# Attention networks of a recurrent mixture kernel: token shift through DRAM, plain transposes, two buffers of the transposed input, feed-forward steps later in the round

## Chip, cores and metric

The kernel runs on one core of a Trainium2 chip. The metric is device time in microseconds (us) from launch to end; lower is better. The kernel before takes 8431.38 us (median of 3 runs, 8424.31 to 8488.79).

## What is computed

Four layers of mixers and feed-forward networks run one after the other on a stream of 8 sequences of 512 tokens with 128 features (4096 tokens in all). The change touches two of the eight networks, both stacks of local attention: L0f (16 heads, 6 layers deep, windows of 32 keys) and L1f (8 heads, 2 layers deep, windows of 64). One layer of either is, cut to what matters:

```python
def shift_tokens(t):                       # half of the features comes from the token before
    a, s = jnp.split(t, 2, -1)
    s = jnp.pad(s, ((0, 0), (1, 0), (0, 0)))[:, :-1]
    return jnp.concatenate([a, s], -1)

x = x + attn_layer(shift_tokens(x), Wqkv, q_scale, k_scale, Wo)
x = x + ffn_layer(shift_tokens(x), ln_g, ln_b, W1, b1, W2, b2)

def attn_layer(x, ...):                    # heads of 64 features
    q, k, v = jnp.split(x @ Wqkv, 3, -1)
    q, k = l2norm(q) * qs, l2norm(k) * ksc
    q, k = rotary(q), rotary(k)            # cos and sin times a position scale
    return local_attention(q, k, v) @ Wo   # a window sees itself and the window before

def ffn_layer(x, g, bln, W1, b1, W2, b2):
    xn = (x - mu) / jnp.sqrt(var + 1e-05) * g + bln
    a, gate = jnp.split(xn @ W1 + b1, 2, -1)
    return a * jax.nn.gelu(gate) @ W2 + b2
```

So each layer shifts tokens twice: the input of the attention, and the input of the feed-forward part.

## The kernel before

The stream of all tokens stays in SBUF as `g.f` (in the profile `f`): 128 partitions (the token within its tile) by 32 tiles by 128 features; a sequence is 4 tiles (`TT = 4`). L0f is `narrow_attention_net`, L1f is `local_attention_net`; their structure is one. Each has three stages: "before" (the first projections), "main" and "after" (the feed-forward part of the last sequence). The main stage makes a round for every layer and sequence: 48 rounds in L0f, 16 in L1f. A round goes over the 4 tiles tt = 0 to 3.

The order of TensorE's work in a round is written out by hand: `ORDER` names the steps of one tile (projections q, k, v; `turn`, the transposes of q and k; `score`, `flip`, the transposes of the probabilities; `value`; `out`, the product with Wo), and `SIDE` names the steps that come once per round and where: `(("fshift",), (0, 1))` puts the step at place 1 of tile 0. Places 0, 1 and 2 of a tile are at its start, after `out` of the tile before, and ahead of `value` of the first group (L0f) or of `flip` (L1f). The orders of VectorE (DVE), ScalarE (ACT) and GpSimd (POOL) are worked out from TensorE's by a small model (`in_order`): a step's `TOOK` moves the clock, and what an engine does for a step is placed at a delay from `LATER` behind it. Each engine then runs its list in order, and semaphores do the rest.

Steps have a lag. `shift`, and the projections of tiles 0 and 1, work for the next sequence; the feed-forward steps `fshift`, `fturn`, `gate` 0 to 2, `up` 0 to 2, `down` work for the sequence before. Products that are read once go through a ring of 3 PSUM banks, given out in the order of use (`Banks`): a step waits until the one three uses earlier has been read.

Token shift for the attention: POOL copies the next sequence from `g.f` to `xb` (L748; step `fetch`). TensorE makes the transposed, shifted input with 12 matmuls (L1005 to L1007; in L1f L1788 to L1790): per tile one with the identity for the features that stay, one with `down1` (a matrix that moves tokens by one place) and one with `last1` (which brings the last token of the tile before). ACT copies the bank to `hT` (L799, L1580), the only buffer, and so waits first until the last projection of the sequence in work has been written. Token shift for the feed-forward part (step `fshift`): three matmuls on `g.f` (L1094 to L1096; L1887 to L1889), which wait for VectorE's addition of `out` of tile 3 (L956, L1739: `f <- ring, f`); VectorE copies the result to `xn` (L961, L1744) and takes its mean and variance with BN_STATS and BN_AGGR; POOL makes `rstd`, ACT normalises `xn` (L854, L1633), TensorE transposes it (`fturn`, L1101, L1894), ACT applies gain and bias into `hnT` (L860, L1639), and the gates follow (L1108, L1901).

SyncE (SP) has the DMA queue. In a round of L0f it issues 30 transfers that gather shifted windows of v into `vmix` (`mix`, L692 to L695): 6 for tile 0, 8 for each other tile. In a round of L1f it issues 6 (L1477, L1478). Each `mix` waits for the projections of v of its tile. SP also loads the weights of the next layer. In the stage "before" it issues rope, mask, ln and wqkv at once, beside POOL's memsets.

## Time and profile before

| | |
|---|---|
| Median of 3 runs | 8431.38 us (8424.31 to 8488.79) |
| Profiled execution, its own time | 8455.97 us |
| Span of its instructions | 8454.1 us |
| L0f, from its first to its last projection copy to hT | 666.1 to 4660.6 us |
| L1f, the same | 5704.6 to 6633.1 us |
| TensorE busy over the span | 80% |
| TensorE clock granted in L0f / in L1f | 0.99 / 0.94 |

How to read it: engine names are PE (TensorE matmul), PEld (its weight load), DVE (VectorE), ACT (ScalarE), POOL (GpSimd), SPq (SyncE's DMA issues). L1018 is line 1018 of the kernel. A fp32 matmul stands in the trace as two instructions, a transpose as one. Busy time of a group is the time in which at least one of it runs, so the sums of lines that alternate (as L1005 to L1007 do) count the same time more than once; a window with only these instructions gives their common time. A granted clock of 1.00 is 2.4 GHz and 0.50 is 1.2 GHz.

### The profile page before, as it was taken

The numbers are of one execution on the slowest core, as the hardware profiler recorded it, in microseconds if no ns is written. First come the engines' busy times: TensorE is split into PE (matmuls) and PEld (weight loads), VectorE is DVE, ScalarE is ACT, GpSimd is POOL, SyncE is SP. The second block draws the span as 40 slices with busy tenths as digits, with TensorE's granted clock in tenths as the row PEclk, the third lists the DMA queues.
The fourth block names the chain that finished last, engine by engine and source line by source line (L and its number), as shares of the span: only waits on it lengthen the run. The fifth ranks groups of instructions, "written<-read, shape, count | busy, mean of one in ns | idle before, by whom it ended". The sixth has DMA issues, their size and how long they took to land. (4 is left out here: it accounts for less than half of the span.)

```text
span 8454.1 us, 243652 instructions
## 1 busy us (share of the span) xinstructions
PE 6789.6 (80%) x92884; PEld 4792.7 (57%) x92884; DVE 5620.9 (66%) x11929; ACT 4975.8 (59%) x10706; POOL 4197.0 (50%) x3732
## 2 busy tenths in 40 slices
PE   5777999999999999999999599987888577633267
PEld 2325666666666666666666488885555323323245
DVE  6895776777677677677677377766667488735332
ACT  4545777777777777777777344436767554302122
POOL 4555665666566566566666245554444355430000
PEclk8888999999999999999999699998999788866578
DMA  3221111111111111111111200000000132321001
GB/s 126 120 98 52 40 41 50 40 38 49 42 41 49 41 38 48 42 41 46 43 41 39 74 5 5 6 13 22 15 23 16 39 146 108 149 68 52 21 0 30
DMA packets 234165, 413.24 MB, mean 49 GB/s; under 512 B 41944, under 2 KB 125360, under 8 KB 214128
## 3 DMA queue, kind: packets, MB, share of 16 engines
q1 hardware_dynamic: 225344, 377.76, 14.2%
q8 instruction: 742, 12.16, 0.6%
q10 hardware_dynamic: 1584, 15.21, 0.4%
q0 software_dynamic: 6144, 5.25, 0.4%
q14 instruction: 351, 2.88, 0.1%
HBM read 208.61 MB, written 32.18 MB: 28 GB/s over the span
## 5 line engine op out<-in xcount | busy, mean ns | idle before, releaser
L763 POOL TENSOR_TENSOR L0f_qr<-L0f_qs,L0f_table 128x512 f32<-128x512 f32 x776 | 989.2, 1275 | 461.9 <-ACT L0f_qs L804 358.9
L1018 PE MATMUL L0f_ring<-L0f_wqkv,L0f_hT 128*128 128x512 f32 x2324 | 1173.3, 611 | 42.2 <-ACT L0f_hT L799 37.5
L770 POOL TENSOR_TENSOR L0f_qr<-L0f_qr,L0f_m 128x512 f32<-128x512 f32 x776 | 984.9, 1269 | 162.2 <-issue 106.5
L834 ACT ACTIVATE L0f_scores<-L0f_scores,L0f_nmx,L0f_rn 128x64 f32<-128x64 f32 x3072 | 982.5, 400 | 132.0 <-DVE L0f_nmx L939 130.8
L1075 PEld LDWEIGHTS L0f_o<-L0f_pT,L0f_vmix 64*64 64x64 f32 x18480 | 759.1, 137 | 158.7 <-issue 136.0
L1075 PE MATMUL L0f_o<-L0f_pT,L0f_vmix 64*64 64x32 f32 x18480 | 801.4, 221 | 50.6 <-ACT L0f_pT L842 31.8
L1075 PE MATMUL L0f_o<-L0f_pT,L0f_vb 64*64 64x32 f32 x6160 | 750.6, 221 | 0.7 <-issue 0.4
L777 POOL TENSOR_TENSOR L0f_qr<-L0f_qr,L0f_rn 128x512 f32<-128x512 f32 x388 | 396.3, 1042 | 687.7 <-DVE L0f_rn L931 686.4
L908 DVE TENSOR_TENSOR L0f_m<-L0f_ring,L0f_table 128x512 f32<-128x512 f32 x776 | 524.0, 685 | 254.9 <-ACT L0f_qs L804 246.3
L1075 PEld LDWEIGHTS L0f_o<-L0f_pT,L0f_vb 64*64 64x64 f32 x6160 | 604.3, 137 | 2.3 <-issue 2.3
L916 DVE TENSOR_REDUCE L0f_ssq<-L0f_sq 128x8 f32<-128x512 f32 x776 | 509.6, 675 | 76.7 <-ACT L0f_sq L809 71.9
L804 ACT ACTIVATE L0f_qs<-L0f_ring 128x512 f32<-128x512 f32 x776 | 474.0, 611 | 140.2 <-PE L0f_ring L1018 131.7
L1018 PEld LDWEIGHTS L0f_ring<-L0f_wqkv,L0f_hT 128*128 128x128 f32 x2324 | 384.7, 191 | 287.5 <-issue 234.4
L1025 PE MATMUL L0f_ring<-const_ident,L0f_qr 128*128 128x128 f32 x3088 | 486.4, 280 | 49.4 <-DVE L0f_m L908 44.5
L850 ACT ACTIVATE L0f_oT<-L0f_o 128x512 f32<-128x512 f32 x385 | 238.1, 618 | 472.6 <-PE L0f_o L1075 472.6
L1025 PEld LDWEIGHTS L0f_ring<-const_ident,L0f_qr 128*128 128x128 f32 x3088 | 355.6, 141 | 282.9 <-issue 184.4
L809 ACT ACTIVATE L0f_sq<-L0f_qs 128x512 f32<-128x512 f32 x776 | 484.9, 646 | 3.6 <-DVE L0f_ssq L916 3.2
L1085 PEld LDWEIGHTS L0f_ring<-L0f_wo,L0f_oT 128*128 128x128 f32 x3088 | 373.3, 197 | 118.9 <-issue 118.9
L2100 POOL TENSOR_TENSOR L0a_dbu<-L0a_du,L0a_bc_all 128x512 f32<-128x512 f32 x256 | 319.7, 1270 | 231.8 <-DVE L0a_da L2218 201.1
L2100 POOL TENSOR_TENSOR L2a_dbu<-L2a_du,L2a_bc_all 128x512 f32<-128x512 f32 x256 | 319.2, 1268 | 231.2 <-DVE L2a_da L2218 199.6
L1085 PE MATMUL L0f_ring<-L0f_wo,L0f_oT 128*128 128x128 f32 x3088 | 393.3, 282 | 0.8 <-ACT L0f_oT L850 0.8
L945 DVE TENSOR_REDUCE L0f_sums<-L0f_scores 128x8 f32<-128x512 f32 x384 | 265.5, 691 | 192.6 <-ACT L0f_scores L834 181.1
(538 smaller groups left out, 17117.0 us busy)
## 6 DMA issues: line engine op xcount, KB each, us to landing
L0f_vmix<-L0f_vb SPq DMA_DIRECT2D x768, 128.0 KB, 2.5
L0a_bc_all<-L0a_bc_rows SPq DMA_DIRECT2D x32, 2048.0 KB, 11.4
L2a_bc_all<-L2a_bc_rows SPq DMA_DIRECT2D x32, 2048.0 KB, 11.3
L0f_vmix<-L0f_vb SPq DMA_DIRECT2D x672, 64.0 KB, 2.0
L1f_vmix<-L1f_vb SPq DMA_DIRECT2D x96, 128.0 KB, 2.4
L0f_wqkv<-L_ffn_wqkv_dram SPq DMA_DIRECT2D x7, 1536.0 KB, 6.2
L2f_parts<-L2f_zero ACTq DMA_DIRECT2D x8, 1088.0 KB, 11.4
n_s<-mixer_out SPq DMA_DIRECT2D x32, 256.0 KB, 5.0
```

The source lines that it names most:

```text
L763: e.tensor_tensor(rotated, qs[:, q % QN], spread(cos, 1, 8), ALU.mult).then_inc(cosed.sem, 1)
L770: e.tensor_tensor(rotated, rotated, m2[:, q % SN], ALU.add).then_inc(added.sem, 1)
L804: e.activation(qs[:, q % QN], ring.at(step)[:], ACT.Copy).then_inc(copied.sem, 1)
L809: e.activation(sq[:, q % SN], qs[:, q % QN], ACT.Square).then_inc(squared.sem, 1)
L834: a = e.activation(s_ps[:, s, h, j], s_ps[:, s, h, j], ACT.Exp, bias=nmx[:, s, col:col + 1], scale=rn[:, tt, 2 * u, col:col + 1])
L908: e.tensor_tensor(m2[:, q % SN].rearrange("p h (a d) -> p h a d", a=2), swapped, spread(sin, 1, 8).rearrange("p h (a d) -> p h a d", a=2), ...
L916: e.tensor_reduce(ssq[:, tt % 2, slot(step)], sq[:, q % SN], AX.X, ALU.add).then_inc(summed.sem, 1)
L1018: e.matmul(bank[:], hT[:, tt * P:tt * P + P], wqkv[:, layer % 2, col:col + 512], start=True, stop=True).then_inc(full, 1)
L1025: a = e.transpose(bank[:, j * P:j * P + P], qr[:, tt % 2, 2 * c + "qk".index(what), 2 * j:2 * j + 2, :], g.ident[:])
L1075: a = e.matmul(o_ps[half, j, cols], values, pT[half, s, j, cols], start=True, stop=True)
L1085: a = e.matmul(bank[:, 0:C], oT[:, tt % 2, j, :], wo[:, j, :], start=j == 0, stop=j == pairs - 1)
L2100: e.tensor_tensor(dbu[:, s], du[:, par, d], bc_all[:, n // QN, 0, n % QN], ALU.mult).then_inc(dbu_ready.sem, 1)
```

## The change

Both networks are changed alike. The shift by one token is no longer made by matmuls: the shifted half of the features goes from SBUF to DRAM (`kept`, one place per sequence, for the attention; `between`, one place, for the feed-forward part) and is read back one row earlier; row 0 is zero. TensorE then makes four plain transposes of `xs` for the attention, and nothing for `fshift`: VectorE takes its statistics from `xf` itself, and ACT normalises from `xf` into `xn`. `hT` has two buffers. `fshift` has no bank of the ring any more (53 uses a round in L0f instead of 54, 33 in L1f instead of 34). The feed-forward steps come later in the round, and in L1f `shift` comes in tile 0 instead of tile 2.

```diff
 # L0f
-    SIDE = [(("fshift",), (0, 1)), (("fturn",), (0, 2)), (("gate", 0), (1, 0)), (("gate", 1), (1, 0)),
-            (("gate", 2), (1, 0)), (("fetch",), (1, 2)), (("up", 0), (1, 1)), (("layer",), (2, 1)), (("shift",), (2, 1)),
-            (("up", 1), (1, 2)), (("up", 2), (2, 2)), (("down",), (3, 2))]
+    SIDE = [(("fshift",), (1, 0)), (("fturn",), (1, 2)), (("gate", 0), (2, 0)), (("gate", 1), (2, 0)),
+            (("gate", 2), (2, 0)), (("up", 0), (2, 1)), (("layer",), (2, 1)), (("shift",), (2, 1)),
+            (("up", 1), (2, 2)), (("up", 2), (3, 0)), (("down",), (3, 2))]
 # L1f
-        SIDE = [(("fshift",), (0, 1)), (("fturn",), (1, 0)), (("gate", 0), (1, 0)), (("gate", 1), (1, 0)),
-                (("gate", 2), (1, 0)), (("fetch",), (0, 2)), (("up", 0), (1, 1)), (("layer",), (2, 1)), (("shift",), (2, 1)),
-                (("up", 1), (1, 1)), (("up", 2), (3, 0)), (("down",), (3, 2))]
+        SIDE = [(("fshift",), (1, 0)), (("fturn",), (1, 2)), (("gate", 0), (2, 0)), (("gate", 1), (2, 0)),
+                (("gate", 2), (2, 0)), (("up", 0), (2, 1)), (("layer",), (2, 1)), (("shift",), (0, 2)),
+                (("up", 1), (2, 2)), (("up", 2), (3, 0)), (("down",), (3, 2))]
 # SP: new functions
+                def keep(s):
+                    e.dma_start(kept[s:s + 1, 1:].rearrange("s (t p) c -> p (s t) c", p=P),
+                                g.f[:, s * TT:s * TT + TT, DH:C]).then_inc(written, 16)
+                def fetch(it, b):
+                    e.wait_ge(*x2_ready(it, ("down",), x2_ready.per))
+                    e.wait_ge(*ring.written(it, ("shift",), 1))
+                    if main and it >= 3:
+                        e.wait_ge(written, 16 * (it - 2))
+                    s = sequence(("shift",), b)
+                    e.dma_start(xs[:, :, 0:DH], g.f[:, s * TT:s * TT + TT, 0:DH]).then_inc(fetched, 16)
+                    e.dma_start(xs[:, :, DH:C], kept[s:s + 1, 0:SEQ].rearrange("s (t p) c -> p (s t) c", p=P)).then_inc(fetched, 16)
+                    if main and it >= 2:
+                        keep((it - 2) % BATCH)
+                def feed_out(it, b):
+                    for done in furthest(*[ring.read(it, ("out", tt), ago(("fshift",), ("out", tt))) for tt in range(TT)]):
+                        e.wait_ge(*done)
+                    e.wait_ge(*xn_ready(it, ("down",), 1))
+                    tile0 = sequence(("fshift",), b) * TT
+                    e.dma_start(between[:, 1:].rearrange("s (t p) c -> p (s t) c", p=P),
+                                g.f[:, tile0:tile0 + TT, DH:C]).then_inc(fed_out, 16)
+                    e.dma_start(xf[:, :, 0:DH], g.f[:, tile0:tile0 + TT, 0:DH]).then_inc(fed_in, 16)
+                def feed_in(it):
+                    e.wait_ge(fed_out, 16 * (it + 1))
+                    e.dma_start(xf[:, :, DH:C], between[:, 0:SEQ].rearrange("s (t p) c -> p (s t) c", p=P)).then_inc(fed_in, 16)
                 if STEPS is BEFORE:
+                    e.wait_ge(zeroed, 1)
+                    e.dma_start(kept[:, 0:1], nought[0:BATCH]).then_inc(written, 16)
+                    e.dma_start(between[:, 0:1], nought[0:1]).then_inc(written, 16)
+                    keep(0)
+                    e.wait_ge(written, 48)
+                    fetch(0, -1)
+                    for s in range(1, BATCH):
+                        keep(s)
                     e.dma_start(rope[:], w["rope"]).then_inc(loaded, 16)
...
-                def mix_all(it):
-                    for tt in range(TT):
-                        mix(it, tt)
+                def mix_all(it, b):
+                    fetch(it, b)
+                    mix(it, 0)
+                    feed_out(it, b)
+                    mix(it, 1)
+                    feed_in(it)
+                    mix(it, 2)
+                    mix(it, 3)
 # ACT
-                            e.activation(hT[:], ring.at(step)[:], ACT.Copy).then_inc(ring.empty_of(step), 1)
+                            e.activation(hT[:, buffer_of(it, step)], ring.at(step)[:], ACT.Copy).then_inc(ring.empty_of(step), 1)
 # DVE, fshift
-                            e.wait_ge(*ring.written(it, step))
-                            e.tensor_copy(xn[:], ring.at(step).rearrange("p (t c) -> p t c", t=TT)).then_inc(ring.empty_of(step), 1)
-                            e.drain()
+                            e.wait_ge(fed_in, 32 * (it + 1))
                             for tt in range(TT):
-                                e.bn_stats(stats[:, tt], xn[:, tt])
+                                e.bn_stats(stats[:, tt], xf[:, tt])
 # PE, shift
-                                e.matmul(bank[0:DH, cols], xb[:, 1 + tt, 0:DH], g.ident[:], start=True, stop=True)
-                                e.matmul(bank[DH:P, cols], xb[:, 1 + tt, DH:C], g.down1[:], start=True, stop=False)
-                                a = e.matmul(bank[DH:P, cols], xb[:, tt, DH:C], g.last1[:], start=False, stop=True)
+                                a = e.transpose(bank[:, tt * P:tt * P + P], xs[:, tt], g.ident[:])
```

(The increments of a semaphore that stand after the waits of SP are left out here. POOL's copy to `xb` and TensorE's three matmuls of `fshift` are removed with their waits. In L1f `mix_all` has no tile 0. `TOOK` of `shift` is 0.5 instead of 1.5 and of `fshift` 0.0 instead of 1.0, which moves the other engines' lists a little. The stage "after" issues `feed_out` and `feed_in` once.)

TensorE in L0f, around the step `out` of the tile before in tile 0 (`L0f_wo,L0f_oT` is `out`, `L0f_wqkv,L0f_hT` a projection), before:

```order
L1018 MATMUL L0f_ring<-L0f_wqkv,L0f_hT 128x512
L1085 MATMUL L0f_ring<-L0f_wo,L0f_oT 128x128 x8
L1094 MATMUL L0f_ring<-f,const_ident 128x4x64
L1095 MATMUL L0f_ring<-f,const_down 128x4x64
L1096 MATMUL L0f_ring<-f,const_last 128x3x64
L1018 MATMUL L0f_ring<-L0f_wqkv,L0f_hT 128x512 x3
L1025 MATMUL L0f_ring<-const_ident,L0f_qr 128x128 x4
```

The same place now:

```order
L1082 MATMUL L0f_ring<-L0f_wqkv,L0f_hT 128x512
L1149 MATMUL L0f_ring<-L0f_wo,L0f_oT 128x128 x8
L1082 MATMUL L0f_ring<-L0f_wqkv,L0f_hT 128x512 x3
L1089 MATMUL L0f_ring<-const_ident,L0f_qr 128x128 x4
```

The three matmuls on `f` are gone, so that the next projections follow `out` at once, with no step of TensorE that waits for VectorE's addition.

VectorE in L0f, at the statistics of the feed-forward part (BN_STATS, BN_AGGR), before:

```order
L956 TENSOR_TENSOR f<-L0f_ring,f 128x128
L961 COPY L0f_xn<-L0f_ring 128x512
L964 BN_STATS L0f_stats<-L0f_xn 128x6 x4
L967 BN_AGGR L0f_mv<-L0f_stats 128x2 x4
L945 TENSOR_REDUCE L0f_sums<-L0f_scores 128x8
L947 RECIPROCAL L0f_sums<-L0f_sums 128x8
L949 TENSOR_TENSOR L0f_prob<-L0f_scores,L0f_sums 128x2x4x64
```

VectorE in L0f at the same instructions now:

```order
L1014 TENSOR_REDUCE L0f_sums<-L0f_scores 128x8
L1016 RECIPROCAL L0f_sums<-L0f_sums 128x8
L1018 TENSOR_TENSOR L0f_prob<-L0f_scores,L0f_sums 128x2x4x64
L1031 BN_STATS L0f_stats<-L0f_xf 128x6 x4
L1034 BN_AGGR L0f_mv<-L0f_stats 128x2 x4
L985 TENSOR_REDUCE L0f_ssq<-L0f_sq 128x8
L977 TENSOR_TENSOR L0f_m<-L0f_ring,L0f_table 128x512
L1006 TENSOR_REDUCE L0f_mx<-L0f_scores 128x8
```

The copy is gone, and the statistics stand at the end of tile 0, behind the probabilities of its second score (the one that `flip` waits for), instead of ahead of those of the first.

SyncE in L0f, a round's new transfers among those of `vmix`, with what each waits for:

```order
L689 DMA L0f_xs<-f 128x4x64 [waits L0f_main_x2_ready,L0f_main_ring2_full,L0f_main_written]
L690 DMA L0f_xs<-L0f_kept 128x4x64
L676 DMA L0f_kept<-f 128x4x64
...
L702 DMA L0f_between<-f 128x4x64 [waits L0f_main_ring0_empty,L0f_main_ring1_empty,L0f_main_xn_ready]
L704 DMA L0f_xf<-f 128x4x64
L757 DMA L0f_vmix<-L0f_vb 32x512 [waits L0f_main_ring0_empty,L0f_main_ring2_empty,L0f_main_ring1_empty,L0f_main_valued]
...
L710 DMA L0f_xf<-L0f_between 128x4x64 [waits L0f_main_fed_out]
```

Before, this queue held only the `vmix` transfers and the weights; now six transfers of 128 KB in pieces of 256 bytes stand in it each round.

## Rows read from the trace of the kernel before

**Rows 1.** The page: span, and busy time by engine.

```profile
span 8454.1 us, 243652 instructions
PE 6789.6 (80%) x92884; PEld 4792.7 (57%) x92884; DVE 5620.9 (66%) x11929; ACT 4975.8 (59%) x10706; POOL 4197.0 (50%) x3732
```

**Rows 2.** Windows: us, busy PE, PEld, DVE, ACT, POOL (instructions), clock, DMA share, GB/s.

```profile
2004.80:3254.60 1249.80, 1167.70 (x19771) 853.80 (x19770) 879.97 (x2018) 963.29 (x2206) 767.99 (x678) 0.99 0.16 43
...
5769.60:6576.40 806.80, 686.53 (x6806) 447.29 (x6805) 554.95 (x1490) 565.33 (x1554) 374.06 (x350) 0.94 0.08 18
...
2041.60:2042.90 1.30, 1.26 (x6) 1.18 (x7) 0.00 (x0) 1.30 (x5) 0.67 (x1) 1.00 0.00 0
6037.00:6042.20 5.20, 5.20 (x7) 1.80 (x8) 1.26 (x2) 3.41 (x5) 2.35 (x2) 0.50 0.00 0
```

**Rows 3.** TensorE's waits, L0f, 754.7 to 4660 us: total us, times, longest.

```profile
PE L0f_scores L1052 <- DVE L0f_prob L949: 66.0, 95, 1.5
PE L0f_ring L1094 <- DVE f L956: 46.6, 47, 2.0
PE L0f_ring L1025 <- DVE L0f_m L908: 37.7, 47, 1.1
PE L0f_ring L1018 <- ACT L0f_hT L799: 36.2, 47, 0.8
PE L0f_o L1075 <- ACT L0f_pT L842: 31.1, 47, 1.0
```

**Rows 4.** Window of one shift in L0f, its instructions alone: us, PE, PEld, POOL, clock.

```profile
2083.16:2085.16 2.00, 1.90 (x24) 1.73 (x24) 0.00 (x0) 1.00 0.00 0
```

**Rows 5.** Timeline of TensorE, L0f: start, us, line, what, count.

```profile
2007.32 0.60 PE L1025 MATMUL L0f_ring<-const_ident,L0f_qr 128*128 128x128 f32 x4
2007.75 0.38 PE L1038 MATMUL L0f_scores<-L0f_mask,ident_bf 128*128 128x256 bf16 x2
...
2056.53 2.74 PE L1108 MATMUL L0f_ring<-L0f_hnT,L0f_w 128*128 128x512 f32 x6
```

**Rows 6.** TensorE's waits, L1f, 5769.6 to 6576.4 us (14 rounds).

```profile
PE L1f_ring L1887 <- DVE f L1739: 17.4, 14, 1.6
...
PE L1f_ring L1901 <- ACT L1f_hnT L1639: 14.6, 14, 1.3
...
PE L1f_ring L1894 <- ACT L1f_xn L1633: 10.5, 14, 1.1
```

**Rows 7.** Timeline of TensorE, L1f: the three gates of one round.

```profile
6036.97 5.39 PE L1901 MATMUL L1f_ring<-L1f_hnT,L1f_w 128*128 128x512 f32 x6 [1.02 <-ACT L1f_hnT L1639]
```

**Rows 8.** Timeline of VectorE, L0f tile 0 and start of tile 1; L1f tile 0.

```profile
2041.22 0.28 DVE L956 TENSOR_TENSOR f<-L0f_ring,f 128x128 f32<-128x128 f32 x1
...
2055.29 0.69 DVE L949 TENSOR_TENSOR L0f_prob<-L0f_scores,L0f_sums 128x512 f32<-128x512 f32 x1
...
2060.32 0.69 DVE L937 TENSOR_REDUCE L0f_mx<-L0f_scores 128x8 f32<-128x512 f32 x1 [1.69 <-PE L0f_scores L1044]
...
6026.97 0.28 DVE L1739 TENSOR_TENSOR f<-L1f_ring,f 128x128 f32<-128x128 f32 x1
```

**Rows 9.** Timeline of SyncE, L0f: the last of tile 1's eight vmix issues.

```profile
2050.48 0.60 SPq L695 DMA_DIRECT2D L0f_vmix<-L0f_vb  x1
```

**Rows 10.** DMA issues: count, KB each, median us to landing.

```profile
L0f_wqkv<-L_ffn_wqkv_dram SPq DMA_DIRECT2D x7, 1536.0 KB, 6.2
...
n_s<-mixer_out SPq DMA_DIRECT2D x32, 256.0 KB, 5.0
...
mixer_out<-L0a_result SPq DMA_DIRECT2D x8, 256.0 KB, 2.3
...
L2f_table<-L2f_wt SPq DMA_DIRECT2D x8, 128.0 KB, 8.6
```

**Rows 11.** Timeline of L0f's stage "before".

```profile
661.64 0.61 POOL L748 COPY L0f_xb<-f 128x512 f32<-128x512 f32 x1 [0.30 <-issue]
...
666.76 5.05 PE L1018 MATMUL L0f_ring<-L0f_wqkv,L0f_hT 128*128 128x512 f32 x10 [0.69 <-ACT L0f_hT L799]
```

More of the change, by code:

```diff
@@ L414, in lag @@
         kind = step[0]
[L415 removed]
+        if kind in ("layer", "shift"):
             return -1
@@ L437, in sequence @@
         return b if lag(step) == 0 else (b - lag(step)) % BATCH
-    TOOK = {"score": 1.5, "value": 1.3, "flip": 1.0, "turn": 0.6, "proj": 0.95, "out": 0.25 * pairs, "shift": 1.5, "fshift": 1.0,
-            "fturn": 0.6, "gate": 0.95, "up": 0.95, "down": 2.8, "fetch": 0.0, "layer": 0.0, "end": 0.0}
+    TOOK = {"score": 1.5, "value": 1.3, "flip": 1.0, "turn": 0.6, "proj": 0.95, "out": 0.25 * pairs, "shift": 0.5, "fshift": 0.0,
+            "fturn": 0.6, "gate": 0.95, "up": 0.95, "down": 2.8, "layer": 0.0, "end": 0.0}
     def in_order(steps, events):
@@ L504, in narrow_attention_net @@
              "unflip_dve": 0.71, "dve_ring": 0.56, "cos": 5.45, "add": 7.38, "kmul": 9.18, "rstd": 0}
-    RING = ("shift", "proj", "turn", "out", "fshift", "fturn", "gate", "up", "down")
+    RING = ("shift", "proj", "turn", "out", "fturn", "gate", "up", "down")
     with ExitStack() as ctx:
@@ L1221, in sequence @@
         return b if lag(step) == 0 else (b - lag(step)) % BATCH
-    TOOK = {"score": 1.5, "value": 1.3, "flip": 1.0, "turn": 0.6, "proj": 0.95, "out": 0.25 * pairs, "shift": 1.5, "fshift": 1.0,
-            "fturn": 0.6, "gate": 0.95, "up": 0.95, "down": 2.8, "fetch": 0.0, "layer": 0.0, "end": 0.0}
+    TOOK = {"score": 1.5, "value": 1.3, "flip": 1.0, "turn": 0.6, "proj": 0.95, "out": 0.25 * pairs, "shift": 0.5, "fshift": 0.0,
+            "fturn": 0.6, "gate": 0.95, "up": 0.95, "down": 2.8, "layer": 0.0, "end": 0.0}
     def in_order(steps, events):
@@ L1296, in local_attention_net @@
                  "unflip_dve": 0.16, "dve_ring": 1.04, "cos": 0.5, "add": 1.57, "kmul": 5.44, "rstd": 1.62}
-    RING = ("shift", "proj", "turn", "out", "fshift", "fturn", "gate", "up", "down")
+    RING = ("shift", "proj", "turn", "out", "fturn", "gate", "up", "down")
     with ExitStack() as ctx:
@@ new lines, in feed_out @@
+                def feed_out(it, b):
+                    for done in furthest(*[ring.read(it, ("out", tt), ago(("fshift",), ("out", tt))) for tt in range(TT)]):
+                        e.wait_ge(*done)
+                        e.sem_inc(passed, 1)
+                    e.wait_ge(*xn_ready(it, ("down",), 1))
+                    e.sem_inc(passed, 1)
+                    tile0 = sequence(("fshift",), b) * TT
+                    e.dma_start(between[:, 1:].rearrange("s (t p) c -> p (s t) c", p=P),
+                                g.f[:, tile0:tile0 + TT, DH:C]).then_inc(fed_out, 16)
+                    e.dma_start(xf[:, :, 0:DH], g.f[:, tile0:tile0 + TT, 0:DH]).then_inc(fed_in, 16)
@@ new lines, in feed_in @@
+                def feed_in(it):
+                    e.wait_ge(fed_out, 16 * (it + 1))
+                    e.sem_inc(passed, 1)
+                    e.dma_start(xf[:, :, DH:C], between[:, 0:SEQ].rearrange("s (t p) c -> p (s t) c", p=P)).then_inc(fed_in, 16)
+                if STEPS is BEFORE:
+                    e.wait_ge(zeroed, 1)
+                    e.sem_inc(passed, 1)
+                    e.dma_start(kept[:, 0:1], nought[0:BATCH]).then_inc(written, 16)
+                    e.dma_start(between[:, 0:1], nought[0:1]).then_inc(written, 16)
+                    keep(0)
+                    e.wait_ge(written, 48)
+                    e.sem_inc(passed, 1)
+                    fetch(0, -1)
+                    for s in range(1, BATCH):
+                        keep(s)
```

181 lines of the change are left out of this document (104 added, 77 removed).

## The prediction, made before the result was known

> **What bounds the kernel now.** I read the page first, for its span and the busy shares [rows 1]: TensorE is at 80%, the highest, but that is a mean over eight networks. Next came windows over the two networks that the change touches [rows 2]. The reader is to see two different pictures. In 15 rounds of L0f, 1249.80 us (83.3 a round), TensorE is busy 1167.70 us, 93%, while ScalarE has 77% and VectorE 70%: TensorE is the bound, and every microsecond taken from it or from its waits should count. In 14 rounds of L1f, 806.80 us (57.6 a round), TensorE is busy 686.53 us, 85%, at a mean clock of 0.94: it also waits, and some of its work runs at 1.2 GHz. Third, the waits of TensorE in either network [rows 3, 6], divided by the rounds of the window (47 and 14); last, timelines of single rounds, to see what stands where.
>
> **TensorE's own work.** The shift for the attention takes 24 instructions in 1.90 us [rows 4]. Four plain transposes take 0.43 us from their start to the start of what follows (2007.32 to 2007.75) [rows 5]. That saves 1.47 us a round. The three matmuls of `fshift` take 1.26 us (window 2041.60:2042.90) [rows 2], all of it removed. Sum: 2.73 us a round, at full clock, in both networks alike, since shapes are the same.
>
> **TensorE's waits that lose their cause.** In L0f `fshift` waits for VectorE's addition, 46.6 us / 47 = 0.99 a round, and the projection behind `shift` waits for the copy to `hT`, 36.2 / 47 = 0.77 [rows 3]. The first wait goes with the instruction; the work behind `out` is a projection that needs only a bank. The second goes because the copy need not wait for the last projection of the old sequence, and in L0f the projection of v that stands between `shift` and k reads the other buffer, so the copy lies beside it. L0f sum: 2.73 + 0.99 + 0.77 = 4.49 us a round, times 48 = 216 us. What is late next: the three other waits, on the probabilities, `m` and `pT`, 66.0 + 37.7 + 31.1 us over 47 rounds, 2.87 a round [rows 3]. Two of them have one occurrence a round, in tile 0, where VectorE's copy and statistics and ScalarE's normalisation stand. The statistics move to the end of tile 0, the normalisation to tile 1, the gates to tile 2. So I expect these waits to move a tile rather than to grow, and count them as unchanged; bounds are 1.3 us a round worse (all of what is not plain work, 1.76, nearly eaten by new ones) and 2 us better.
>
> In L1f the wait for the addition is 17.4 / 14 = 1.24, for `xn` 10.5 / 14 = 0.75, for `hnT` 14.6 / 14 = 1.04 [rows 6]. The last two stand there because `fturn` and the gates come back to back at the start of tile 1; now a half tile or more lies between the links. And the three gates, six instructions, take 5.39 us [rows 7] at a clock of 0.50 [rows 2], against 2.74 us in L0f at full clock for the same shapes [rows 5]: 2.65 us a round that a TensorE kept busy ahead of them would not pay. Sum: 2.73 + 1.24 + 0.75 + 1.04 + 2.65 = 8.41 a round. I take 6.5, because L1f's tiles are short and its other waits have less cover; bounds 2.7 (plain work alone) and 9.5. Times 16: 104 us (43 to 152).
>
> The Trainium skill, "TensorE: Matmul & The Clock Gate", Part 4, says that transposes do not count as busy for the clock gate. The low clock in L1f stands behind a stretch of waits and transposes, which agrees; by that rule the 2.65 us could stay, since `fturn` and `flip`, both transposes, still come right ahead of the gates. It is a rival below.
>
> **What the new transfers cost.** No row shows 128 KB in 512 pieces of 256 bytes. The nearest are 256 KB in pieces of 512 bytes: SBUF to DRAM 2.3 us, DRAM to SBUF 5.0 [rows 10]; I take 3.5, bounds 2.3 and 8.6 (the slowest row of 128 KB, eight in a queue). Issues cost 0.60 each [rows 9]. The chain that could be late is the feed-forward one, in L0f: the addition ends at 2041.50 [rows 8]; two issues; `mix` of tile 1, eight issues, whose last ended at 2051.08 before [rows 9]; then the issue of the read back, which lands at 2051.1 + 2.3 to 5.0 = 2053.4 to 2056.1. VectorE wants it behind the probabilities, which end at 2055.98 [rows 8] less the 2.25 us that the tile gets shorter: 2053.7. So it waits 0 to 2.4 us there, and has 1.69 us of idle ahead of its next maximum [rows 8] as cover. Queued behind it are VectorE's `ssq`, `m` and the maximum of the next score, for which ScalarE's exponentials and TensorE's `flip` wait. I count nothing. In L1f the addition ends at 6027.25 [rows 8], both transfers in turn with their issues take 7 to 9 us, so about 6035; tile 1 begins at 6036.97 [rows 7] less 1.26 + 1.24 + 0.75 + 1.04 = 6032.7. A wait of up to 2 us is part of what I took off 8.41.
>
> SyncE now holds `mix` of tile 0 behind `fetch`, which waits for the end of the feed-forward part of the round before. That part ends with `down` at place 2 of tile 3, and `vmix` is used behind place 2 of the next tile 0, a quarter of a round or 20 us later [rows 2]; three plus six issues of 0.60 and a landing make 8 to 10 us: hidden. `fetch` itself has two tiles (L0f) or most of one (L1f). POOL's copy is 0.61 us a round [rows 11] on an engine at 61% [rows 2]: nothing either way.
>
> **Stage starts and ends.** The first projection of L0f starts at 666.76, 5.1 us behind POOL's copy to `xb` at 661.64 [rows 11]. Now, after the memsets: three issues, a landing, two issues, a landing (1.8 + 2.3 + 1.2 + 3.5 = 9 us), and wqkv is issued only behind these, seven `keep` and three loads, ten issues or 6 us later, with 6.2 us to landing [rows 10]: 661.3 + 5.3 + 6 + 6.2 = 679. That is 12 us later; L1f, with half the weights, 10. The stage "after" has two transfers in a row instead of three matmuls and a copy: 5 to 8 us, twice. In all +35 us (15 to 60).
>
> **Sum.** -216 - 104 + 35 = -285 us. Against the profiled execution, 8455.97 us (span 8454.1 and 1.9 around it), that gives 8171; this execution was 24.6 us above the median of 8431.38, for which the forecast is 8146 us.
>
> **Rivals.**
> 1. The waits come back elsewhere: VectorE and ScalarE must do nearly the same in less time, and only TensorE's plain work is gained. For it: ScalarE would be at 64.2 us in a round of 79. Against it: tiles without side steps show almost no waits. -2.73 x 64 + 35 = -140: 8291 us.
> 2. L1f's clock stays down at the gates or falls elsewhere, through transposes and short waits: 2.65 x 16 = 42 us are not gained: 8188 us.
> 3. The waits of tile 0 go as well, as the copy and the late addition caused them: 2 us x 48 more: 8050 us.
> 4. TensorE was not the bound and all that is taken from it turns to idle; only the starts are felt: 8466 us. The 93% speaks against it.
> 5. Slower: the read back through DRAM is late in every round. It decides from a landing of about 8 us each way, where L0f still gains a little (from the issue's end at 2042.1 to 2053.7 + 1.69 + 4.49 = 2059.9 there is time for two landings of 8.6 and an issue) and L1f loses. At 10, VectorE would stand until 2062.7 in L0f, 9.0 us less 1.69 of cover less 4.49 gained, +2.8 x 48 = 135; in L1f until 6027.25 + 21.2 = 6048.5, 15.8 less 6.5, x 16 = 149; with 35 that is 8750 us. For it: the slowest row of this size shows 8.6; against it: that row has eight in a queue.
>
> The Trainium skill, "DMA: Bandwidth & Descriptors", Specifications, says that a piece under 512 bytes is read and modified before it is written, which every new transfer would pay; no row here shows such a pair. This is why rival 5 is not left out.
>
> **How the numbers follow.** Forecast 0.40, rival 1 0.20, rival 2 0.20, rival 3 0.09, rival 4 0.06, rival 5 0.05. The range 8060 to 8300 holds the forecast with its own bounds (8090 to 8215), rivals 1 and 2 and the edge of 3. A measurement of this kernel tells about 1% (84 us) from no change: the forecast and rivals 1 to 3 are faster by more, 0.89; rival 4 is within it, 0.06; rival 5 slower, 0.05.
>
> **What would show it.** In the profile after: a round of L0f at 78.8 us and TensorE at 95% there or more; no wait of TensorE for `f` ahead of the feed-forward part and none for `hT`; three gates of L1f in 2.7 us at a clock of 1.00; a round of L1f near 51 us; VectorE's wait for the transfer to `xf` under 1 us. Wrong would be: the three other waits growing beyond 3 us a round, VectorE held by the transfer, or a low clock in L1f at another place.

## The result and the profile after

| | before | after |
|---|---|---|
| median, us (runs) | 8434.28 (9) | 8521.72 (9) |
| lowest to highest, us | 8424.31 to 8488.79 | 8513.36 to 8538.01 |
| span of the profiled execution, us | 8454.1 | 8530.8 |

The changed kernel is slower: ratio 1.0105, 95% interval 1.0093 to 1.0116, some 87 us. The forecast was 8146 us, its range 8060 to 8300. Ratios of the experiments below are to runs of the kernel before that were taken beside them (medians 8433.88 to 8441.21).

The page of the kernel after, its span and busy times, beside [rows 1]:

```profile
span 8530.8 us, 241066 instructions
PE 6675.0 (78%) x91104; PEld 4635.1 (54%) x91168; DVE 5614.3 (66%) x11863; ACT 4965.8 (58%) x10706; POOL 4159.9 (49%) x3666
```

TensorE lost 115 us of work, as intended, and the span grew by 77. So it now waits more. Where: first the windows (us, busy PE, PEld, DVE, ACT, POOL, clock, DMA share, GB/s), the first over the same stretch of L0f as in [rows 2], the second over 14 rounds of L1f, from the addition that ends one round to the fourteenth after it:

```profile
2004.80:3254.60 1249.80, 1139.50 (x19153) 811.34 (x19151) 876.49 (x1985) 951.49 (x2180) 750.17 (x652) 0.97 0.20 52
5862.00:6684.60 822.60, 648.16 (x6395) 417.87 (x6456) 535.54 (x1477) 562.95 (x1554) 366.31 (x337) 0.94 0.13 31
```

TensorE in L0f is at 91%, not 95% or more, and its clock is lower, 0.97 against 0.99. Then the copies to `hT`, whose first and last start give the length of the 48 rounds. They are 84.49 us each (4722.0 less 666.7, over 48); before, the same line ran from 666.1 to 4660.6, 83.22 each. Forecast were 78.8.

```profile
L867 ACT ACTIVATE L0f_hT<-L0f_ring x49: 597/645/650, 666.7 to 4722.0; 128x512 f32<-128x512 f32 x49
```

The first of these intervals begins in the stage "before" and holds the start of the network. The first copy of the main stage stands at 772.5 after and at 759.6 before, so 12.9 us of the 61 are the start, and the 47 rounds behind it take 84.03 us each, before 83.00.

L1f has to be read by another line, since the change also moved its `shift` from tile 2 to tile 0, and the copies to `hT` with it. The last addition of a round, to `f`, stayed in its place. Its first and last start, before and after:

```profile
L1766 DVE TENSOR_TENSOR f<-L1f_y,f x17: 693/1117/1393, 5787.3 to 6691.4; 128x512 f32<-128x512 f32 x17
```

```profile
L1885 DVE TENSOR_TENSOR f<-L1f_y,f x17: 693/1103/1126, 5862.0 to 6781.9; 128x512 f32<-128x512 f32 x17
```

904.1 us before, 919.9 after: L1f's 16 rounds are a microsecond longer each. By these marks the 77 us stand so: up to L0f's last addition +65, between it and L1f's first `hT` nothing, L1f to its last addition +26, the rest -14.

Third, TensorE's waits in L0f, 754.7 to 4722 us, which answer to [rows 3] (total us, times, longest):

```profile
PE L0f_ring L1082 <- DVE f L1025: 121.9, 47, 3.7
PE L0f_scores L1116 <- DVE L0f_prob L1018: 75.2, 88, 1.2
PE L0f_ring L1082 <- ACT L0f_vb L886: 31.5, 41, 0.8
PE L0f_o L1139 <- ACT L0f_pT L910: 30.2, 38, 1.1
PE L0f_ring L1082 <- ACT L0f_hT L867: 27.1, 47, 0.6
...
PE L0f_ring L1089 <- ACT L0f_vb L886: 23.6, 41, 0.6
PE L0f_ring L1089 <- DVE L0f_m L977: 12.7, 41, 0.6
```

The first line is the finding. The name is the one of before, VectorE's addition to `f`, but it is another wait. Before, `fshift` read the sum in tile 0, and that wait is gone. Now a projection (L1082) in tile 1 only wants the bank of the ring in which `out` had put its result, and gets it when the addition has read it. 121.9 us in 47 rounds are 2.6 a round. So it is not the case that no step of TensorE waits for VectorE's addition any more, as the section on the change has it. The waits for `vb`, the copies of v, are new too: 31.5 + 23.6 us, 1.2 a round, in tile 0 where `fshift` stood.

### The profile page after: what moved, and what is told of

The parts are those of the page before. It is cut to its first block and busy times, and to the rows that moved or that the text cites. A ratio compares the mean times of both kernels' runs of the same rounds, so it can differ in the third digit from the quotient of the medians.

```text
span 8530.8 us, 241066 instructions
## 1 busy us (share of the span) xinstructions
PE 6675.0 (78%) x91104; PEld 4635.1 (54%) x91168; DVE 5614.3 (66%) x11863; ACT 4965.8 (58%) x10706; POOL 4159.9 (49%) x3666
## 5 line engine op out<-in xcount | busy, mean ns | idle before, releaser
L1082 PE MATMUL L0f_ring<-L0f_wqkv,L0f_hT 128*128 128x512 f32 x2324 | 1213.3, 622 | 200.1 <-DVE f L1025 125.3
L1082 PEld LDWEIGHTS L0f_ring<-L0f_wqkv,L0f_hT 128*128 128x128 f32 x2324 | 376.0, 193 | 447.5 <-DVE f L1025 165.0
L985 DVE TENSOR_REDUCE L0f_ssq<-L0f_sq 128x8 f32<-128x512 f32 x776 | 511.3, 677 | 82.6 <-ACT L0f_sq L877 71.8
L1089 PE MATMUL L0f_ring<-const_ident,L0f_qr 128*128 128x128 f32 x3088 | 512.0, 291 | 47.3 <-ACT L0f_vb L886 23.6
L1089 PEld LDWEIGHTS L0f_ring<-const_ident,L0f_qr 128*128 128x128 f32 x3088 | 366.6, 146 | 313.1 <-issue 206.8
```

The costliest lines, as they stand in the source:

```text
L985: e.tensor_reduce(ssq[:, tt % 2, slot(step)], sq[:, q % SN], AX.X, ALU.add).then_inc(summed.sem, 1)
L1082: e.matmul(bank[:], hT[:, buffer_of(it, step), tt * P:tt * P + P], wqkv[:, layer % 2, col:col + 512], start=True, stop=True).then_inc(full, 1)
L1089: a = e.transpose(bank[:, j * P:j * P + P], qr[:, tt % 2, 2 * c + "qk".index(what), 2 * j:2 * j + 2, :], g.ident[:])
```

## The wait followed back: tile 1 of L0f

TensorE, timeline (start, us, line, what; in brackets the idle time before it and what ended it):

```profile
2085.76 1.84 PE L1149 MATMUL L0f_ring<-L0f_wo,L0f_oT 128*128 128x128 f32 x15
2087.43 1.88 PE L1082 MATMUL L0f_ring<-L0f_wqkv,L0f_hT 128*128 128x512 f32 x4
2091.43 1.12 PE L1082 MATMUL L0f_ring<-L0f_wqkv,L0f_hT 128*128 128x512 f32 x2 [2.12 <-DVE f L1025]
```

`out` is done at 2087.6, the addition comes at 2091.08. What VectorE does in between:

```profile
2080.93 0.86 DVE L1031 BATCH_NORM_STATS2 L0f_stats<-L0f_xf 128x6 f32<-128x128 f32 x4
2081.87 0.38 DVE L1034 BATCH_NORM_AGGREGATE L0f_mv<-L0f_stats 128x2 f32<-128x6 f32 x4
2082.37 0.69 DVE L985 TENSOR_REDUCE L0f_ssq<-L0f_sq 128x8 f32<-128x512 f32 x1
...
2086.07 1.10 DVE L996 SCALAR_TENSOR_TENSOR L0f_est<-L0f_rn 128x32 f32<-128x32 f32 x1
2087.25 0.19 DVE L998 TENSOR_TENSOR L0f_est<-L0f_est,L0f_ssq 128x32 f32<-128x32 f32 x1
2087.51 1.15 DVE L1000 SCALAR_TENSOR_TENSOR L0f_rn<-L0f_est,L0f_rn 128x32 f32<-128x32 f32 x1
2088.73 0.19 DVE L996 SCALAR_TENSOR_TENSOR L0f_est<-L0f_rn 128x32 f32<-128x32 f32 x1
2089.00 1.10 DVE L998 TENSOR_TENSOR L0f_est<-L0f_est,L0f_ssq 128x32 f32<-128x32 f32 x1
...
2091.08 0.29 DVE L1025 TENSOR_TENSOR f<-L0f_ring,f 128x128 f32<-128x128 f32 x1
```

Two things. The statistics, which the change put at the start of tile 1, take 1.44 us ahead of everything else; and three of the Newton steps take 1.10 to 1.15 us where their like take 0.19. Beside them GpSimd:

```profile
2082.70 1.04 POOL L850 TENSOR_TENSOR L0f_rstd<-L0f_rstd,L0f_half 128x4 f32<-128x4 f32 x1
...
2084.43 1.26 POOL L831 TENSOR_TENSOR L0f_qr<-L0f_qs,L0f_table 128x512 f32<-128x512 f32 x1
2085.86 1.27 POOL L838 TENSOR_TENSOR L0f_qr<-L0f_qr,L0f_m 128x512 f32<-128x512 f32 x1 [0.16 <-issue]
2087.34 1.27 POOL L831 TENSOR_TENSOR L0f_qr<-L0f_qs,L0f_table 128x512 f32<-128x512 f32 x1 [0.22 <-issue]
2088.77 1.28 POOL L838 TENSOR_TENSOR L0f_qr<-L0f_qr,L0f_m 128x512 f32<-128x512 f32 x1 [0.16 <-issue]
```

Each long step starts inside one of GpSimd's 1.27 us instructions and ends within 0.05 us of that one's end (2087.17 and 2087.13, 2088.66 and 2088.61, 2090.10 and 2090.05). GpSimd is there at that time because the normaliser (2082.36 to 2084.47), also moved to tile 1, stands ahead of its four long instructions. The Trainium skill, "SBUF — State Buffer", "Who interferes with whom", says that a VectorE instruction with two SBUF inputs contends with a GpSimd instruction that reads SBUF: the trace agrees. It says too that one with at most one SBUF input does not, outside VectorE's 2-port modes. Of such instructions the trace shows both. The reductions keep their 0.68 us beside a running GpSimd instruction (L985 at 2084.41), but TENSOR_SCALAR L991, `ssq <- ssq`, took 0.55 us at 2085.18 and ended with GpSimd's at 2085.7, where it takes 0.18 with GpSimd idle. Whether it ran in such a mode no run here tells.

The lines of VectorE before and after (busy us, mean ns) show it over all of L0f:

```profile
L939 DVE SCALAR_TENSOR_TENSOR L0f_nmx<-L0f_mx,L0f_rn 128x8 f32<-128x8 f32 x376 | 233.5, 621 | 29.3 <-issue 1.7
L931 DVE SCALAR_TENSOR_TENSOR L0f_rn<-L0f_est,L0f_rn 128x32 f32<-128x32 f32 x567 | 109.1, 192 | 45.7 <-issue 4.5
```

```profile
L1000 DVE SCALAR_TENSOR_TENSOR L0f_rn<-L0f_est,L0f_rn 128x32 f32<-128x32 f32 x567 | 154.4, 272 | 44.6 <-issue 3.0
L1008 DVE SCALAR_TENSOR_TENSOR L0f_nmx<-L0f_mx,L0f_rn 128x8 f32<-128x8 f32 x378 | 146.3, 387 | 28.5
```

Collisions were there before as well, on `nmx` (621 ns against 170 where it is alone), where they hid. There they cost less now (146.3 us instead of 233.5), but they fall on the Newton steps ahead of the addition too, on each of their three lines as on L1000.

The wait has a second price. In windows of 3 us of another round, which has the wait of 2.82 us up to 2514.69:

```profile
2512.00:2515.00 3.00, 0.31 (x1) 0.31 (x2) 2.62 (x8) 0.57 (x1) 1.76 (x2) 0.83 0.33 87
2515.00:2518.00 3.00, 3.00 (x12) 1.39 (x11) 2.16 (x5) 0.94 (x2) 2.79 (x3) 0.50 0.58 158
2518.00:2521.00 3.00, 3.00 (x74) 2.83 (x74) 1.98 (x4) 3.00 (x8) 2.68 (x3) 0.53 0.11 29
```

Behind it TensorE works at 1.2 GHz (0.50) for some 6 us. The wait of 2.12 us at 2091 has no such stretch behind it: the clock is 1.00 up to 2097. In all of L0f 44 waits for the addition are longer than 2 us. By the trace's record of the granted clock, a stretch at 1.2 GHz, mostly shorter than this one, begins beside the end of 30 of them. The shortest of the 30 is 2.13 us, and the longest of the other 14 is 2.75, so the length of a wait does not tell.

## Experiments

Theory 1: the later places of the feed-forward steps cost, through the order on VectorE and GpSimd in tile 1. Rivals: SyncE's queue, where mixing now stands behind the new transfers (theory 2); and the way through DRAM. A round of L0f below is always (last less first start of the copy to `hT`) / 48: 83.22 us before, 84.49 after. In every kernel with the way through DRAM this holds 9 to 13 us of a longer start, 0.2 to 0.3 a round, which the kernel before and the one with the places alone do not have.

**Statistics behind the addition.** On the changed kernel:

```diff
-    SIDE = [(("fshift",), (1, 0)), (("fturn",), (1, 2)), ...
+    SIDE = [(("fshift",), (1, 1)), (("fturn",), (1, 2)), ...
-             ..., "kmul": 9.18, "rstd": 0}
+             ..., "kmul": 9.18, "rstd": 3.0}
```

> The changed kernel, with only L0f's VectorE and GpSimd order altered: the statistics of the feed-forward input stand behind the addition of `out` in tile 1 instead of ahead of the Newton steps, and the normaliser's four small GpSimd instructions stand behind `kmul`. Theory 1 (VectorE's order): TensorE's wait for a ring bank that VectorE's addition frees, 121.9 us in 47 rounds, falls below 40 us, the rows of est and rn fall from 0.27 back to 0.19 us, and the time falls by 80 to 125 us, to 8400 to 8440 us. Theory 2 (SyncE's queue: mixing stands behind the new transfers): nothing of that order changes, 8520 us, and the wait stays, merely under another name.

Measured: 8397.87 us, ratio to before 0.9955 (0.9938 to 0.9971), 2 us under the range of theory 1. A round 81.80 us. The line for `f` is gone from TensorE's waits and the Newton steps are back at 193 ns:

```profile
L1000 DVE SCALAR_TENSOR_TENSOR L0f_rn<-L0f_est,L0f_rn 128x32 f32<-128x32 f32 x561 | 108.0, 193 | 45.6 <-issue 4.9
```

Every engine executes the same instructions as in the changed kernel; 124 us hang on the place of a dozen of them (four BN_STATS and four BN_AGGR of VectorE, four of GpSimd). TensorE's order is the same to the instruction. Theory 2 falls: SyncE's order was not touched.

**Only the normaliser later.**

```diff
-             ..., "kmul": 9.18, "rstd": 0}
+             ..., "kmul": 9.18, "rstd": 8.8}
```

> The changed kernel with one thing altered: in L0f GpSimd's four instructions of the normaliser (1.9 us) stand behind `kmul`; VectorE's order is as changed, the statistics still ahead of tile 1's Newton steps. It tells how the 2.6 us a round divides. If the Newton steps are late because GpSimd's long instructions, pushed back by 1.9 us, hold VectorE's two-input instructions (three rows of 1.10 to 1.15 instead of 0.19 us: 2.8 us), these rows are gone, TensorE's wait for the addition falls to about 1 us a round and the time to 8430 to 8460. If it is the 1.3 us of statistics alone, little changes: 8500 to 8520.

Measured: 8475.52 us, 1.0046 (1.0031 to 1.0061), a round 83.41, between the two expectations. The Newton steps are at 0.193 us though the statistics still stand ahead of them, and the wait for the addition fell from 121.9 to 13.2 us. So the collisions made nine tenths of it. About half of what that gave back went into a new wait, as the normaliser is now late for `fturn`, and TensorE was at 1.2 GHz for 246 us instead of 191 (754.7 to the last copy to `hT`). The waits of this run, 754.7 to 4673 us:

```profile
PE L0f_ring L1154 <- ACT L0f_xn L923: 57.0, 47, 1.6
...
PE L0f_ring L1082 <- DVE f L1025: 13.2, 18, 1.5
```

**The places alone.** The kernel before, with L0f's table of the changed one (and `fetch` where it was):

```diff
-    SIDE = [(("fshift",), (0, 1)), (("fturn",), (0, 2)), (("gate", 0), (1, 0)), ...
+    SIDE = [(("fshift",), (1, 0)), (("fturn",), (1, 2)), (("gate", 0), (2, 0)), ...
```

> The kernel before with one part of the change alone: L0f's feed-forward steps at the later places, shift and feed shift still by matmuls, POOL's copy still there. Theory 1: it is the places that cost. VectorE's copy of 0.69 us and the statistics stand ahead of tile 1's Newton steps, the addition is late as in the changed kernel, nothing is gained: +2.6 us or more a round, 8530 to 8600 us. If the places are neutral and the way through DRAM is what costs, it is at 8434 us within 20.

Measured: 8630.54 us, 1.0234 (1.0217 to 1.0251), a round 86.99. More than expected; the wait for the bank is there without any transfer:

```profile
PE L0f_ring L1018 <- DVE f L956: 116.3, 47, 2.9
```

The places cost 197 us, 180 of them up to L0f's last addition (4912.8 us, before 4732.8). The changed kernel stands 109 below this run. And `fshift` with its bank is still there in this run, so the wait in tile 1 does not come from its removal.

**The attention's shift alone.** In L0f: shift through DRAM, plain transposes, two buffers of `hT`; `fshift` by matmuls, all feed-forward steps in their old places. L1f as before. Against the changed kernel, in L0f, cut:

```diff
+    SIDE = [(("fshift",), (0, 1)), (("fturn",), (0, 2)), (("gate", 0), (1, 0)), ...
-                    feed_out(it, b)
-                    feed_in(it)
+                            e.tensor_copy(xn[:], ring.at(step).rearrange("p (t c) -> p t c", t=TT))...
```

> The kernel before with the other part of the change alone, in L0f: the attention's shift through DRAM, four plain transposes and two buffers of hT; the feed-forward shift is still three matmuls, its steps at their old places, L1f as before. If the shift itself gains what was forecast for it, 1.47 us of plain work and 0.77 of the wait for hT a round: -2.2 x 48 = -107, and +12 for the start: 8340 us (8310 to 8380). The run with the places alone stands 109 us above the changed kernel, which says the same for both shifts together. If ScalarE's late copies of v eat it, as they do in tile 0 of the changed kernel, about half is left: 8390.

Measured: 8341.70 us, 0.9881 (0.9864 to 0.9899), a round 81.03, which is 2.19 less than before, for 2.24 expected (2.44 less without the start: 80.56 against 83.00). This is the fastest version of the study, 180 us below the changed kernel. Its waits, to 4560 us:

```profile
PE L0f_ring L1133 <- DVE f L998: 46.5, 47, 2.0
PE L0f_ring L1064 <- DVE L0f_m L950: 37.9, 47, 1.1
PE L0f_o L1114 <- ACT L0f_pT L884: 30.8, 47, 1.0
...
PE L0f_ring L1057 <- ACT L0f_hT L841: 13.9, 48, 0.3
```

**Old places, earlier read back.** The changed kernel with L0f's steps near their old places:

```diff
+    SIDE = [(("fshift",), (0, 2)), (("fturn",), (1, 0)), (("gate", 0), (1, 0)), ...
-                    mix(it, 1)
                     feed_in(it)
+                    mix(it, 1)
```

> The changed kernel with L0f's feed-forward steps back at the places of before (statistics at place 2 of tile 0, since they need the transfer), and the read back of the shifted half issued ahead of the mixing of tile 1, so that mixing is 1 to 3 us later. Theory 1: the statistics no longer stand ahead of tile 1's Newton steps, TensorE's wait for the addition goes to under 1 us a round; unless the normalisation is then late for `fturn`, the time is 8360 to 8430 us. Theory 2: mixing is later still, ScalarE waits for it and the time is 8520 us or more. If `fturn` waits for `xn` by 1 to 3 us a round, 8430 to 8500.

Measured: 8674.35 us, 1.0283 (1.0262 to 1.0303), a round 87.12: none of the three. The wait for the addition is gone, and mixing is later without harm (ScalarE waits for no transfer, and TensorE 31.6 us for `vb` at L1082, 31.5 in the changed kernel). Instead TensorE waits 198.0 us for `m`, and VectorE for GpSimd, and TensorE's mean clock in the window of [rows 2] is 0.95. VectorE's wait, 754.7 to 4851.8 us:

```profile
DVE L0f_m L977 <- POOL L0f_qr L838: 231.1, 47, 5.2
```

GpSimd stood in front of the normaliser until the statistics came (190.2 us in 47 rounds), with the rotation of the queries queued behind it. The same kind of cause as theory 1, on the other engine of the pair.

**ScalarE's copy of v ahead of the exponentials**, on the run with the statistics behind the addition:

```diff
-    LATER = {"exp": 2.38, ...
+    LATER = {"exp": 2.42, ...
```

> The run with the statistics behind the addition, and ScalarE's copy of v in each tile of L0f ahead of the first exponential instead of behind it. Theory: TensorE waits for these copies 55 us in 47 rounds (31.5 and 23.7), because fshift no longer stands between `out` and the projections of tile 0 as cover, while ScalarE stands before its first exponential until VectorE's maximum is there. Then these two waits fall below 15 us and the time to 8350 to 8370. Rival: the wait only moves (exponentials 0.5 us later in every tile, TensorE waits for probabilities): 8390 to 8420.

Measured: 8411.38 us, 0.9965 (0.9952 to 0.9978), a round 81.96. The rival: the wait at L1082 went, and those for `hT` (27.1 to 54.0 us) and for `vb` at L1089 (23.7 to 45.7) took its place.

**A filler where fshift stood.** On the same run:

```diff
+                            if main and tt == TT - 1:
+                                e.matmul(bank[:], hT[:, buffer_of(it, proj(1, "v", 1)), P:2 * P],
+                                         wqkv[:, (0 if l is None else l) % 2, 0:512], start=True, stop=True)
                             for j in range(pairs):
```

> The run with the statistics behind the addition, and in every round of L0f one more projection-sized matmul (two instructions, 0.95 us, its result overwritten) ahead of `out` in tile 0, near where fshift stood. Theory: there TensorE waits for ScalarE's copies of v anyway, 1.2 us a round, so fshift's removal from that place gained nothing: the waits for vb fall from 55 to under 20 us in 47 rounds and the time rises by less than 15 us, to 8398 to 8413. Rival: its plain work counts in full, 0.95 x 48 = 46: 8444 us.

Measured: 8432.96 us, 0.9995 (0.9985 to 1.0004), 35 us above the run without it, so the total misses the theory's range. But L0f did not take them: its copies to `hT` ran from 666.5 to 4593.0 with the filler and from 666.8 to 4593.1 without, a round 81.80 both. In the profiled execution 48 matmuls of 0.95 us cost nothing there. The wait for `vb` at L1082 went from 31.5 to none, which is 0.67 of the 0.95 (that at L1089 stayed, 23.3, so the two are not under the 20 expected). The clock gave the rest: TensorE was at 1.2 GHz for 96 us instead of 116, by an estimate 0.2 a round. The profiled executions are 17 us apart (8417.0 and 8399.9), and the difference arises between L0f's last addition and L1f's first `hT`, 995.9 against 974.2 us, in a network whose code is the same. Why this one took longer wasn't found. The profiled execution is also the fastest of ten, whose median is 14 us higher, and where those lose more no trace shows.

**fshift behind the projection of v**, with the attention's shift alone in both networks (the last run of this section); VectorE, ScalarE and GpSimd keep their order:

```diff
-             ("side", 1), ("v", 0), ("k", 0), ...
+             ("side", 1), ("v", 0), ("side", 3), ("k", 0), ...
```

> As the run with the attention's shift alone in both networks, and in L0f TensorE's fshift stands behind the projection of v instead of ahead of it, VectorE's and GpSimd's order unchanged. In that run TensorE still waits 46.5 us in 47 rounds for the addition ahead of fshift. If that wait can be covered by the projection: -0.99 x 48 = -47, near 8280 us. If it only becomes a wait for v's bank, as when fshift was taken out: the same time within 10 us.

Measured: 8387.73 us, 0.9945 (0.9929 to 0.9962), 30 above the run with fshift in its old place, which neither expectation had; a round 81.63 against 81.01. The wait for the addition became two for `vb` (34.4 and 10.1) and a longer one for `m` (37.1 to 56.0):

```profile
PE L0f_ring L1064 <- DVE L0f_m L950: 56.0, 47, 1.6
PE L0f_ring L1133 <- ACT L0f_vb L860: 34.4, 41, 1.8
```

**L1f.** First its full change alone:

> L1f changed in full, L0f as before. By the two traces L1f's rounds took the same time (928.5 and 927.3 us) and the stages around it a little longer: 8434 to 8455 us. Were L1f the cause of the loss, it would be near 8520; were it a gain that L0f hides, below 8400.

Measured: 8462.67 us, 1.0036 (1.0022 to 1.0050), 29 above before and 8 above the range expected. The expectation rested on the copies to `hT`, which had moved within the round; by the last addition the run has 916.5 us for L1f's rounds, 12 more than before, and 10 more ahead of the first of them. L1f lost, and did not merely fail to gain. Its waits of TensorE, from 5789 us, 14 or 15 rounds, to be held against [rows 6]:

```profile
PE L1f_ring L1946 <- ACT L1f_xn L1701: 36.0, 14, 2.7
PE L1f_ring L1864 <- ACT L1f_vb L1666: 26.3, 18, 2.0
PE L1f_ring L1953 <- DVE L1f_m L1755: 20.7, 14, 1.5
```

All three are new or longer. The wait for `vb` is in tile 0 where `fshift` stood, as in L0f. The one for `xn` was tried, on the run with the statistics behind the addition:

```diff
-                 "square": 3.84, ..., "xn": 0,
+                 "square": 3.84, ..., "xn": 3,
```

> The run with the statistics behind the addition, and in L1f ScalarE's normalisation 3 us earlier among the exponentials of tile 1. In the changed kernel TensorE waits there for xn 35.8 us in 14 rounds, 2.6 a round, in place of the two waits of before. If that wait was what ate L1f's gain: under 0.5 us a round, -2 x 16 = -32: 8365 us. If four exponentials are then late for `flip` (the normalisation takes 1.7 us), it stays at 8398.

Measured: 8391.85 us, 0.9946 (0.9928 to 0.9963), against 8397.87. The wait went from 38.5 us to none, that for the probabilities rose from 22.5 to 37.1 and one for `m`, 17.0, took its place: 6 us of 32, and the intervals of the two ratios overlap, so even these are not clear of the noise.

Then the attention's shift alone in both networks:

> The attention's shift through DRAM with plain transposes and two buffers of hT in both networks; the feed-forward shift by matmuls and all feed-forward steps at their old places, in both. L0f alone gave 8341.7 us, 2.19 us a round. If L1f gains its 1.47 us of plain work too, -1.5 x 16 = -24 and +10 for its start: 8328 us (8310 to 8345). If L1f's tiles give nothing for less work of TensorE, as with the full change: 8342 to 8360.

Measured: 8358.04 us, 0.9909 (0.9893 to 0.9926). L0f is as with L0f alone (81.01 a round), L1f's rounds took 910.7 us (first to last addition) against 900.5 in the run with L1f as before. Even the plain work is not gained in L1f. There a projection waits longer for a bank that the addition of `out` holds, 31.5 us in 14 rounds against 14.0 in the run with L1f as before:

```profile
PE L1f_ring L1878 <- DVE f L1819: 31.5, 28, 2.3
```

## Why the prediction was wrong

The rounds of L0f can be added up from the traces, from the first copy to `hT` of the main stage to the last, 47 rounds. Plain work is the prediction's; waits are TensorE's idle time there. Time lost to the low clock is an estimate: half of the time that the granted clock was 0.50. In us a round against before:

| | after | statistics behind the addition | attention's shift alone |
|---|---|---|---|
| plain work of TensorE | -2.73 | -2.73 | -1.47 |
| waits, the loads of `ln` left out | +2.20 | +0.33 | -0.65 |
| clock (at 1.2 GHz for 191, 116 and 58 us; before 68) | +1.30 | +0.50 | -0.11 |
| sum | +0.77 | -1.90 | -2.23 |
| measured | +1.03 | -1.65 | -2.44 |

The sums are within 0.3 us of what was measured.

Step by step:

- "TensorE's own work", 2.73 a round: the size is right, in L1f too (below). With the attention's shift alone its part came out in L0f (1.47 of work, and 0.47 of the 0.77 for `hT`; in the changed kernel the wait for `hT` only fell from 36.2 to 27.1 us, 0.19 a round). fshift's 1.26 did not come out: it stood in tile 0 where TensorE then waits for ScalarE's copies of v. The filler bears this out for 0.7 of its 0.95, and moving fshift by one place brought waits for the same copies.
- "The first wait goes with the instruction; the work behind `out` is a projection that needs only a bank." The wait did go, but "needs only a bank" failed: the banks behind `out` come free with ScalarE's copies of v, and the projections and `turn` wait 1.2 us a round for them, more than the 0.99 that was to be saved. In tile 1 the third use of the ring behind `out`, the projection of q, needs the bank that the addition frees; that was so before, and cost nothing while the addition came in time.
- "I expect these waits to move a tile rather than to grow, and count them as unchanged." This is the step that failed by most in L0f: 2.6 us a round where nothing was put. Three waits were followed, and the prediction wrote down where the moved steps land, but not what stands behind them on VectorE and GpSimd in tile 1. The moved statistics (1.4 us) and normaliser (2.1 us) pushed Newton steps and GpSimd's long instructions onto each other, and the addition behind them: 2.6 us a round in place of the bound of 1.3. Both runs that move the normaliser alone or with the statistics take this wait away (to 13.2 us and to none) with `fshift` absent all the same; the run with the places alone has it with `fshift` present. The wrong-if line, "three other waits beyond 3 us a round", looked for known waits (2.5 a round) where a new one came.
- The clock: the prediction looked for a low one in L1f alone. It fell in L0f, mostly beside the waits for the addition, by an estimate 1.3 us a round, and no term of the sum had that. In the run with the statistics behind the addition, too, there are such stretches; 17 of its 23 stand behind a wait of about 1 us for `pT`, as that of 2222 to 2228 us (0.68 and 0.75). What makes them there was not tried.
- L1f, -6.5 a round forecast, +1 measured. TensorE is not the bound there. In 14 rounds it had 38 us less to do than in [rows 2] (648.16 against 686.53), 2.7 a round as forecast, and the 14 rounds took 822.60 us instead of 806.80. Each wait taken away came back as another. "Its other waits have less cover" was written in the prediction and priced at a quarter; it was worth all. This step failed as well, and the bound of 2.7 with it. Rival 4 came true in this network, and its rounds even grew; against it the prediction had only the 93% of the other. Which of the moved steps makes them grow is open: moving the normalisation alone left the time within the noise.
- Rival 2 named L1f for the low clock, and half of it came. The three gates of a round took 2.74 to 4.38 us, 4.07 at the median of 16, instead of 5.39; those shown below begin at 1.2 GHz and end at 2.4. The mean clock stayed at 0.94, so the low stretches lie elsewhere in the round, and what the gates gained did not shorten it.

```profile
6184.99 3.61 PE L2006 MATMUL L1f_ring<-L1f_hnT,L1f_w 128*128 128x512 f32 x6
```

- Rivals 1 and 3 were faster than before and fell with the rounds. Rival 5 fell. The new transfers land faster than the 3.5 us assumed. Count, KB each, median us to landing:

```profile
L0f_xs<-L0f_kept SPq DMA_DIRECT2D x49, 128.0 KB, 2.8
L0f_between<-f SPq DMA_DIRECT2D x49, 128.0 KB, 1.9
...
L0f_xf<-L0f_between SPq DMA_DIRECT2D x49, 128.0 KB, 2.2
```

  VectorE waited for the read back 22.0 us in 37 rounds, 0.6 each, under the microsecond forecast. What the Trainium skill says of pieces under 512 bytes ("DMA: Bandwidth & Descriptors", Specifications), that they are read and modified before they are written, was why rival 5 had a chance; it doesn't show as a longer landing in these medians.
- Starts and ends, +35: this term was about right. L0f's first projection begins at 678.08 us, forecast 679, before 666.76:

```profile
678.08 6.09 PE L1082 MATMUL L0f_ring<-L0f_wqkv,L0f_hT 128*128 128x512 f32 x10 [11.40 <-issue]
```

  The first of the additions that end a round came 14 us later (801.7 against 788.1). In L1f it came 92.6 us behind the first copy to `hT` instead of 82.7, 10 later as forecast. Only the two ends were smaller, 3.0 and 0.3 us longer instead of 5 to 8 each. Together they are 27 us. What follows L1f's last addition took 14 us less, but that is hardly the change: it took 1749 and 1753 us in the two kernels with L1f as before, 1748.8 in the changed one and 1762.7 before. The stretch between the two networks varied by 31 us from kernel to kernel (965.1 to 995.9), so totals a few tens of us apart say little by themselves.

## What to carry to other kernels

- When a step goes from one engine's order, ask what its time covered. Here the steps behind it waited 1.2 us a round for copies that had been done in time before. And in a rotating set of buffers look up whose reading frees the next one, and what could delay that reader.
- When small instructions are moved onto an engine in mid-round, list what they push there and on its neighbour, up to the instruction that frees something. A busy share says nothing of that: here 70% and 60% in L0f.
- In L0f, at a busy share of 93%, 2.24 us a round of work and wait taken from TensorE with the other steps at their places gave 2.19; in L1f, at 85% and with waits on many instructions of VectorE and ScalarE, neither 1.47 taken that way nor 2.7 in the full change gave anything. Price the second kind by what is left when its waits come back.
